# Letting the second, third and fourth scatter of a batch each wait for one of VectorE's maxima

## What is computed

```python
x = _layernorm(x + attn(x))        # gated linear attention, two heads of 64
x = _layernorm(x + xattn(x, ctx))  # 16 heads; for each token one context row is picked by argmax,
                                   # its key and value take part in a softmax over the token's rows
x = _layernorm(x + ffn(x))         # mixture of experts: 16 experts, the best 4 of each token
```

```python
logits = x @ router_w + router_b
topw, topi = top_k(softmax(logits), 4)
```

## Time and profile before

| | |
|---|---|
| time, median of 3 runs | 814.66 us (809.4 to 816.93) |
| the profiled execution's own time | 810.59 us |
| its span, first to last instruction | 808.4 us |
| mean granted TensorE clock in it | 0.767 of full speed |
| busy: TensorE, VectorE, ScalarE, GpSimd | 74%, 56%, 49%, 49% of the span |

### The profile page before, as it was taken

One profiled execution on the slowest core, in us unless ns is written; L12 is line 12 of the kernel. 1 busy time (PEld: TensorE's weight loads), 2 busy tenths in 40 slices (PEclk: granted clock), 3 DMA queues, 4 the chain that ended last, 5 costly groups with the idle time before them and its releaser, 6 DMA issues.

```text
span 808.4 us, 17516 instructions
## 1 busy us (share of the span) xinstructions
PE 601.7 (74%) x4222; PEld 484.3 (60%) x4222; DVE 454.1 (56%) x1551; ACT 392.6 (49%) x1124; POOL 399.1 (49%) x496
## 2 busy tenths in 40 slices
PE   5687876875798888888898613788767777777395
PEld 2465555654576666666675412677757776666374
DVE  4788996565555555555566467444444444434276
ACT  4576894464444444444454302444444445444226
POOL 3766551112334444444455573555555555565392
PEclk8988998598755656655656655988898889888688
DMA  5000100116532222222111123222222222222292
GB/s 170 24 19 14 35 2 19 42 40 171 144 99 61 60 59 56 59 60 59 52 49 53 47 70 98 71 70 73 74 72 71 74 75 75 63 75 66 88 383 80
DMA packets 88395, 60.01 MB, mean 74 GB/s; under 512 B 39292, under 2 KB 78850, under 8 KB 88096
## 3 DMA queue, kind: packets, MB, share of 16 engines
q1 hardware_dynamic: 78496, 42.12, 19.0%
q0 software_dynamic: 8704, 16.87, 6.4%
q10 hardware_dynamic: 1152, 0.53, 0.2%
HBM read 33.10 MB, written 23.21 MB: 70 GB/s over the span
## 4 chain that ended last, share of the span: by engine, by line
PE 55%; DVE 16%; issue 11%; another core or an unknown queue 7%; ACT 5%; DMA 3%; POOL 1%; SPq 1%; DVEq 0%; ACTq 0%; POOLq 0%
PE bank L911 12%; PE bank L918 10%; PE bank L903 6%; PE bank L747 5%; PE bank L721 3%; PE bank L738 3%; PE bank L939 2%; DVE mx L1384 2%; PE bank L713 2%; PE bank L682 1%; PE bank L846 1%; ACT hid L1182 1%; DVE Rq L1279 1%; PE bank L759 1%
## 5 line engine op out<-in xcount | busy, mean ns | idle before, releaser
L592 POOL DMA_INDIRECT ys<-yout,xin x144 | 143.0, 993 | 123.3 <-DVE yout L1597 80.7
L911 PE MATMUL bank<-xinT,wcur 128*128 128x128 f32 x584 | 113.5, 326 | 62.7 <-ACT xinT L1175 58.6
L566 POOL DMA_INDIRECT xs<-xrow,slots x128 | 127.3, 994 | 42.8 <-issue 42.8
L911 PEld LDWEIGHTS bank<-xinT,wcur 128*128 128x128 f32 x584 | 93.1, 227 | 76.8 <-ACT xinT L1175 66.0
L1384 DVE TENSOR_REDUCE mx<-bank 128x4 f16<-128x308 f32 x128 | 61.2, 478 | 129.1 <-remote 65.2
L1182 ACT ACTIVATE hid<-bank,wcur 128x128 f32<-128x128 f32 x292 | 91.0, 364 | 78.4 <-PE bank L911 64.5
L1597 DVE TENSOR_TENSOR yout<-bank,wcur 128x128 f32<-128x128 f32 x144 | 41.8, 290 | 125.4 <-PE bank L918 101.8
L556 POOL TENSOR_TENSOR bd<-src,bmask 101x308 f16<-101x308 f16 x32 | 22.2, 695 | 169.3 <-DVE w L1407 126.5
L918 PE MATMUL bank<-wcur,hid 128*128 128x128 f32 x576 | 103.3, 310 | 0.0
L1085 ACT ACTIVATE Ex<-bank 77x512 f32<-77x512 f32 x128 | 72.6, 588 | 52.8 <-remote 29.3
L918 PEld LDWEIGHTS bank<-wcur,hid 128*128 128x128 f32 x576 | 92.2, 228 | 0.0
(11 more groups left out here) (214 smaller groups left out, 1263.9 us busy)
## 6 DMA issues: line engine op xcount, KB each, us to landing
xin<-xs SPq DMA_DIRECT2D x156, 64.5 KB
yin<-ys SPq DMA_DIRECT2D x16, 512.0 KB
qs<-qtrip SPq DMA_DIRECT2D x96, 32.0 KB
ys<-yout,xin POOLq DMA_INDIRECT x144
xTg<-xT_dram SPq DMA_DIRECT2D x8, 256.0 KB, 2.9
X<-x_dram SPq DMA_DIRECT2D x1, 2048.0 KB, 9.3
x1s<-X SPq DMA_DIRECT2D x32, 64.0 KB, 1.8
qtrip<-qhl SPq DMA_DIRECT2D x32, 64.0 KB
```

Source lines behind the costliest of these rows:

```text
L566: pool.indirect_dma_start(words, bass.IndirectOffsetOnAxis(ap=slots[p][:, r:r + 1], axis=0), xrow[p][:, r, 0:RW], None).then_inc(s(f"scatt ...
L592: pool.indirect_dma_start(ys, bass.IndirectOffsetOnAxis(ap=xin[p][:, :].bitcast(U32)[:, E:RW], axis=0), yout[p][:, :], None, bounds_check= ...
L911: mm = pe.matmul(psH[p % 3][:, c * P:(c + 1) * P], wcur[p % QUAD][:, c * P:(c + 1) * P], xinT[p % 4][:, :], start=True, stop=True)
```

## The change

Three of the four scatters of a batch get a wait. For r = 1, 2 and 3, GpSimd waits until `mx_ready` has reached 4*(b+7) + r, that is until m0, m1 and m2 of batch b+7 are done: with b = t-6 in GpSimd's step t, those are the maxima of batch t+1, the ones that VectorE takes at that time. `pause` is an increment of a semaphore that nobody waits for. Where a batch t+1 doesn't exist, at the end, nothing is waited for, so the steps with the waits are those in which GpSimd issues `scatter` and `keys` both (25 steps). Nothing is removed, and the order of each queue stays.

```diff
-            def scatter(i, c):
+            def scatter(i, c, ahead=0):
 
                 b, p = 4 * i + c, c % 4
                 pool.wait_ge(s("row_to"), b + 1)
                 pool.wait_ge(s("slots_ready"), b + 1)
                 pause(pool)
                 for r in range(TOP):
+                    if ahead and r >= 1:
+                        pool.wait_ge(s("mx_ready"), NQ * (b + ahead) + r)
+                        pause(pool)
                     pool.indirect_dma_start(...)
...
                 if there(i, c - 6):
-                    scatter(i, c - 6)
+                    scatter(i, c - 6, 7 if there(i, c + 1) else 0)
                 if there(i, c - 3):
                     row_numbers(i, c - 3)
```

## The result

The changed kernel takes 773.4 us (median of 4 runs, 769.1 to 775.3) against 814.5; the ratio is 0.951, 95% interval 0.947 to 0.955. That is 41 us, where 22 were forecast. The profiled execution has a span of 770.9 us (808.4 before) and a mean granted clock of 0.826 (0.767 before). L724, L709, L849, L1387, L1367, L1408 and L569 are L721, L706, L846, L1384, L1364, L1405 and L566 of the kernel before.

What follows compares the result with a forecast made beforehand. TensorE's work plus its wait for increments made late by close scatters was taken as the bound. Terms 21.3 + 1.2 + 1.5 - 0.5 - 0.5 = 23.0, 22 kept, gave 792 us; own range 782 to 801, overall 766 to 818.

Steps and rivals of the forecast that it cites:

- The bound: Steps from 219.05 to 395.93 us: TensorE's work plus 1.34 us a step idle before L721, from increments late during close scatters.
- Lone scatters let increments through: Spaced scatters in each step: increments falling into a lone issue come promptly, delay taken near 0 for g2 and g3.
- The "slower" rival: Each scatter holds back the increment the next waits for: +16 us over 17 steps, 830 us; chance 0.14.
- 17 steps x 1.25 us: Main gain, steps from 219.05 to 395.93 us: each falls from 10.40 to 9.15 us, 21.3 us in all.
- the clock as a rival: Granted clock rises from 0.61 to 0.81 as gaps close; step 7.6 us, stage loses 48 us: 766; chance 0.13.
- a clock outside 0.55 to 0.7: Sign that the prediction is wrong: the granted clock, 0.61 in these steps, leaves 0.55 to 0.7.
- 0.24 us for each wait: GpSimd's step: price of each added wait and pause, taken from L1407's end at 385.29 to L556's start at 385.53.
- What is late next is nothing but TensorE's own queue.: Step at 386 us: with m1 done by 391.0, g2 starts at 391.2 instead of 392.75, behind L706 only.
- half is given back: Rival: g3's and L846's increments arrive 0.99 us after s3's end; about 10 us gained, 804; chance 0.17.
- The end of the burst: Close scatters: some increments arrive only when the burst is over; m1 starts 0.99 us after the last issue ended.
- the 0.5 us for the end: Loss of 0.5 us: s3 of the last step with waits comes later, with a burst behind it that lets m3 go.
- The 1.2 us for the step at 209 us: Gain of 1.2 us in the step at 209 us, which has the same wait as the 17 steps.

Runs made afterwards that it cites:

- run 3: Kernel before plus a 256-column memset and a wait for it ahead of the second, third and fourth scatter, chip A: 781.0 us, ratio 0.960.
- run 1: Changed kernel with its three waits put on the maxima of the batch before, always already met, chip A: 818.9 us, ratio 1.005.
- run 2: Kernel before plus 14 small unused fp16 matmuls ahead of g2, scatters untouched, chip A: 804.8 us, ratio 0.989.
- Five scatters: Kernel before plus one copied scatter ahead of each batch's four: 840.7 us, ratio 1.034 on chip C; 691.4 us, ratio 1.059 on B.
- run 8: Changed kernel with only the third scatter's wait, plus 256-column memsets ahead of the second and fourth scatter, chip B: 657.9 us, ratio 1.008.

## Why the prediction came out as it did

**The bound.** Right: late increments, and TensorE's wait before g2. The changed kernel has 0.30 us of idle time before L724 a step, where "under 0.3" was forecast from 1.34, and no remote wait of m1 is left.

**Lone scatters let increments through.** Right, and it decided the sign. The step at 322 us shows it, run 3 shows it for all 17 steps, and run 1 shows that it is nothing else in the change. The "slower" rival falls. One of the two rows that I cited for it was misread: the increment at 511.28 falls 0.04 us behind the end of the lone scatter (511.24), not into it. The step at 322 us has what that row lacks: g1 ends at 325.92, inside s1's issue of 325.48 to 326.44, and m1 starts at 325.96. Nor did VectorE's L1367 hold up s2 much, as it ends at 326.89 and s2 starts only at 327.32: 0.88 us after m1's end, where s1 and s3 start 0.82 and 0.81 after the ends of m0 and m2.

**The term that was mis-sized: 17 steps x 1.25 us.** It measured 1.75, 29.8 us in place of 21.3, and the five later steps gave 7.0 in place of 1.5. In both it is TensorE's busy time that fell, by 33.4 and 9.9 us, while its idle time rose, by 3.6 and 3.0. I took the distance to the 9.15 us of the later steps, and 1.34 us of idle time as the upper bound, which holds only while the clock stays at 0.61. I had the clock as a rival, at 0.13 and 766 us, and judged by the busy share that density decides nothing. It went to 0.79, while that share fell from 87% to 82%, and run 2 shows that filling this one gap is enough for such a rise. The prediction had named a clock outside 0.55 to 0.7 as a sign that it was wrong, and this sign came. So the gain of 41 us for 22 is not luck in the direction, but the path by which most of it came was the rival's. The measured 773.4 lies outside the forecast's own range of 782 to 801 and nearer to that rival; what the rival had too low was the idle time left, 0.8 us against 1.59.

**0.24 us for each wait.** Wrong: a wait that isn't met yet costs about 0.8 us from the event to the next issue. m0 ends at 324.66 and s1 starts at 325.48; run 3 has 0.82 behind its memset. It was priced from the start of L556, which is another kind of instruction. It did no harm by itself, as it makes distance, but with the shorter steps it used up GpSimd's cover inside a pair.

**"What is late next is nothing but TensorE's own queue."** Wrong in every second step: the rival "half is given back" had the place, g3 and L846. There m3 is 2.7 to 3.0 us late, and ScalarE's L1106, which reads L798 and lets L849 start, waits on "remote" too, 13.0 us in five of the steps. It comes about because the faster steps meet the maxima before GpSimd asks for them, so the waits space nothing.

**The end of the burst.** I read from 14 of 17 steps that m1 waits for it. Five scatters speak against this: 2.7 us again in 13 of 17 steps. A fixed delay of 2.7 us fits these, but neither the 3.4 to 4.2 us in the other four nor the 2.0 to 2.3 us in four steps of the kernel before. What exactly holds an increment, and what lets it go, stays open.

**Small terms.** From the start of the last `keys` with waits to the end, the span has 367.2 us now and 366.7 before, so the 0.5 us for the end was right. The 1.2 us for the step at 209 us was right as well: the first of the 17 steps starts at 217.82 instead of 219.05.

## What to carry to other kernels

When a consumer starts on a "remote" release long after its producer ended, look at what else runs at that moment in every step, and then vary that thing alone; here the distance between GpSimd's indirect DMAs was worth 5%. If closing a gap would make TensorE's work denser, put the time at the next clock level into the forecast's own range, not beside it. Pace by something that still paces when the kernel is faster, and measure on more than one chip before keeping such a repair. And once a cause is known, look for it in the other stages too: there the view may not say "remote".

## What the runs showed of the hardware

- The same kernel took 812 and 814 us on two chips and 652 and 651 on two others. The latter's traces, of altered kernels, have no late increment of the maxima in the cross stage, with scatters 0.30 us apart. Of the 160 us between them some 64 lie in the expert stage.
- On the former, an increment of TensorE beside four scatters 0.30 us apart came mostly 2.7 us late and up to 3.0, up to 4.2 beside five, and once 5.6 in a row of eight; in the changed kernel's steps with all scatters 0.8 us and more apart each maximum started within 0.05 us of its matmul's end.
- 14 small fp16 matmuls in one gap of 1.6 us per step took the mean granted clock of the stage from 0.61 to 0.82.
- GpSimd's next indirect DMA starts 0.8 us after the event that its wait was for, and 0.30 us behind the last one if the wait is already met.
- In the expert stage of the kernel before, 55 of 128 readers of L903 started more than 0.5 us late; in run 8 on B none of 130 did, and the stage took 189.5 us instead of 253.8.
